# Attention with experts on one core: the experts' transposes and logits in the maxima's banks, P V in pairs of key blocks

## What is computed

```
xq, xk, xv = x @ wq.T, x @ wk.T, x @ wv.T          # (4, 1024, 16, 32)
probs = softmax(einsum('bqhd,bkhd->bhqk', xq, xk))
x = layernorm(x + (probs @ xv) @ wo.T)
logits = x @ Wr.T + br;  p = softmax(logits);  e = argmax(p)
h = einsum('nd,erd->ner', x, A);  y = einsum('ner,eor->neo', h, B) / 64
x = layernorm(x + y[e] * max(p))
```

## Time and profile before

| | us |
|---|---|
| median of three executions | 1601.32 |
| the profiled execution | 1602.13 |
| its span, first to last instruction | 1600.2 |
| TensorE busy | 1520.6 (95%) |
| POOL busy | 1184.0 (74%) |
| VectorE busy | 999.9 (62%) |
| ScalarE busy | 772.8 (48%) |

### The profile page before, as it was taken

How to read it: one execution, slowest core, us unless ns; L and a number is a source line. 1 busy time by engine, 2 the same in 40 slices (tenths; PEclk the granted TensorE clock), 3 DMA queues, 4 the chain that set the end, 5 groups by cost and what they waited for, 6 DMA issues and landing times.

```text
span 1600.2 us, 20249 instructions
## 1 busy us (share of the span) xinstructions
PE 1520.6 (95%) x6816; PEld 836.2 (52%) x6816; DVE 999.9 (62%) x1764; ACT 772.8 (48%) x1421; POOL 1184.0 (74%) x655
## 2 busy tenths in 40 slices
PE   6798979999999999999999999999999999999898
PEld 5664436666545555555644554555654444453354
DVE  5575576665586766656568667665556776672433
ACT  3154545555455454455545454544554545555222
POOL 0087889899977768777788876678877888889601
PEclk9898989999999999999999999999999999999999
DMA  7933334545232332237342133333433222210001
GB/s 230 295 99 97 99 105 139 153 140 142 84 99 64 83 93 76 71 100 221 96 146 47 58 89 87 83 110 104 171 90 100 48 47 58 57 41 21 7 1 53
DMA packets 79287, 156.27 MB, mean 98 GB/s; under 512 B 19008, under 2 KB 25168, under 8 KB 78800
## 3 DMA queue, kind: packets, MB, share of 16 engines
q1 hardware_dynamic: 77520, 152.33, 33.4%
q0 software_dynamic: 608, 2.12, 0.4%
q10 hardware_dynamic: 1056, 0.52, 0.1%
HBM read 105.66 MB, written 48.49 MB: 96 GB/s over the span
## 4 chain that ended last, share of the span: by engine, by line
PE 79%; DVE 8%; DMA 4%; issue 3%; SPq 2%; POOL 2%; ACT 1%; ACTq 0%; POOLq 0%; DVEq 0%
PE w L566 16%; PE sc L684 14%; PE pv L696 13%; PE mx L674 13%; PE w L643 5%; PE w L630 5%; PE w L601 5%; DVE mxc L885 3%; PE mx L655 2%; DMA stack<-qk_parts 2%; DVE xT_s L902 1%; PE w L623 1%; DVE gate L995 1%; DVE eq L990 1%; SPq L344 1%
## 5 line engine op out<-in xcount | busy, mean ns | idle before, releaser
L885 DVE TENSOR_REDUCE mxc<-mx 128x1 f32<-128x512 f32 x1024 | 680.7, 685 | 449.2 <-PE mx L674 447.5
L770 ACT ACTIVATE P<-sc 128x512 f32<-128x512 f32 x1024 | 594.6, 596 | 607.7 <-PE sc L684 592.5
L501 POOL TENSOR_TENSOR Psum<-Psum,P 128x1024 f32<-128x1024 f32 x300 | 711.0, 2396 | 45.7 <-ACT P L770 42.3
L684 PE MATMUL sc<-stack 98*128 98x512 f32 x1024 | 547.2, 536 | 7.7 <-ACT P L770 3.8
L674 PE MATMUL mx<-stack 96*128 96x512 f32 x1024 | 409.4, 403 | 26.5 <-DMA stack<-qk_parts 15.9
L684 PEld LDWEIGHTS sc<-stack 98*128 98x128 f32 x1024 | 195.3, 191 | 202.1 <-ACT P L770 94.8
L696 PE MATMUL pv<-P,V 128*32 128x512 f32 x2048 | 274.4, 608 | 0.0
L674 PEld LDWEIGHTS mx<-stack 96*128 96x128 f32 x1024 | 197.5, 193 | 130.8 <-issue 57.4
L566 PE MATMUL w<-xT_s,wqk_s 128*128 128x512 f32 x768 | 227.6, 411 | 20.8 <-DVE xT_s L902 13.2
L498 POOL TENSOR_TENSOR Psum<-P 128x1024 f32<-128x1024 f32 x50 | 117.8, 2376 | 147.8 <-PE mx L655 113.8
L566 PEld LDWEIGHTS w<-xT_s,wqk_s 128*128 128x128 f32 x768 | 144.2, 194 | 93.2 <-issue 55.2
(11 more groups left out here) (125 smaller groups left out, 1017.6 us busy)
## 6 DMA issues: line engine op xcount, KB each, us to landing
stack<-qk_parts SPq DMA_DIRECT2D x192, 256.0 KB, 5.5
qk_parts<-split SPq DMA_DIRECT2D x64, 512.0 KB, 3.2
wqk_s<-wqk_parts SPq DMA_DIRECT2D x30, 512.0 KB, 4.9
xT_s_f<-xT SPq DMA_DIRECT2D x8, 1024.0 KB, 11.2
den_s<-den_parts SPq DMA_DIRECT2D x124, 64.0 KB, 2.0
r<-x SPq DMA_DIRECT2D x3, 2048.0 KB, 9.4
out<-r SPq DMA_DIRECT2D x12, 512.0 KB, 3.9
wide<-wv_parts SPq DMA_DIRECT2D x2, 2048.0 KB, 12.0
```

Of the source, the lines that this page charges most:

```text
L501: pool.tensor_tensor(sums(s)[:, i, :], sums(s)[:, i, :], P[:, unit % NP, :], ALU.add).then_inc(add_done, 1)
L684: pe.matmul(sc[c][:, :], stack(s, i)[0:KS, 0, 128 * kb:128 * kb + 128], stack(s, i)[0:KS, 1, 512 * c:512 * c + 512], start=True, stop=True ...
L770: act.activation(P[:, unit % NP, 512 * c:512 * c + 512], sc[c][:, :], ACT.Exp).then_inc(exp_done, 1)
L885: dve.tensor_reduce(mxc[:, q % 2, m:m + 1], mx[TURN[g] % NMX][:, :], AX.X, ALU.max).then_inc(mx_done, 1)
```

## The change

Three edits, made together.

- **P V in pairs.** A new function `blocks(s, k)` says which key blocks are issued in unit k. In all slots but 7 it is two blocks in every fourth unit: blocks 0 and 1 in half 11, 2 and 3 in half 19, 4 and 5 in half 27, 6 and 7 in half 3 of the next slot. Slot 7 keeps one block every second unit.
- **Banks.** `t1`, `t2` and `lg` (`SHORT`) leave the order of the two `w` banks and take turns in the three `mx` banks. A turn now waits for whoever frees the turn three before: VectorE (`mx_done`), or ScalarE's copy after a `t1` or `t2`, or VectorE's bias add after a `lg`. The closing stage is as before.
- **Order of a tile's steps.** Before: lg, h, z of the tile before, t1 of the next, t2, then the projections. Now: z of the tile before, t2, lg of the next, projections, h of the next, t1 of the one after.

```diff
+    SHORT = ("t1", "t2", "lg")
...
-        pieces = [("t1", at)] + take(0) + [("lg", at), ("h", at), ("t1", at + 1)] + take(1) + [("t2", at)]
+        pieces = [("t1", at)] + take(0) + [("lg", at), ("h", at), ("t1", at + 1)] + take(1)
         for t in range(KB):
-            if t + 1 < KB:
-                pieces += [("lg", at + t + 1), ("h", at + t + 1)]
-            pieces += ([("z", at + t)] if t + 1 < KB else [])
-            if t + 2 < KB:
-                pieces.append(("t1", at + t + 2))
-            if t + 1 < KB:
-                pieces.append(("t2", at + t + 1))
-            pieces += take(t + 2)
+            pieces += ([("z", at + t - 1)] if t else []) + [("t2", at + t)]
+            pieces += ([("lg", at + t + 1)] if t + 1 < KB else []) + take(t + 2)
+            pieces += ([("h", at + t + 1)] if t + 1 < KB else []) + ([("t1", at + t + 2)] if t + 2 < KB else [])
         return pieces + fill + [("z", at + KB - 1)]
...
-        ORDER += PLAN[s]
+        ORDER += [piece for piece in PLAN[s] if piece[0] not in SHORT]
...
+    def next_turn(what):
+        TURN[what], FREES[what] = len(TURNS), frees + (what[0] not in SHORT)
+        TURNS.append(what)
+        return FREES[what]
...
         if s and h == den_at(s):
-            TURN["den", s - 1], turn = turn, turn + 1
-    TURNS = turn
+            frees = next_turn(("den", s - 1))
+        for kind, n, _ in AT.get(half, ()):
+            if kind in SHORT:
+                frees = next_turn((kind, n))
+
+    def blocks(s, k):
+
+        if s == PAIRS - 1:
+            return ((k - 3) // 2,) if k % 2 and k >= 3 else ()
+        return ((k - 5) // 2, (k - 3) // 2) if k % 4 == 1 and k >= 5 else ()
...
+        for turn, piece in enumerate(TURNS):
+            BANK[piece] = mx[turn % NMX]
...
+            def take_turn(what):
+
+                turn = TURN[what]
+                if turn >= NMX:
+                    old, n = TURNS[turn - NMX]
+                    if old in SHORT:
+                        pe.wait_ge(FREED_BY[old], n + 1)
+                    else:
+                        pe.wait_ge(mx_done, FREES[old, n])
+                return BANK[what]
+
             def begin(piece, last):
+                if not last and piece[0] in SHORT:
+                    return take_turn(piece)
...
-                if c == 1 and k == 1 and s:
-                    out_block(s - 1, KB - 1)
-                if c == 1 and k % 2 == 1 and k >= 3:
-                    out_block(s, (k - 3) // 2)
+                if c == 1 and s:
+                    for kb in blocks(s - 1, UNITS + k):
+                        if kb < KB:
+                            out_block(s - 1, kb)
+                if c == 1:
+                    for kb in blocks(s, k):
+                        out_block(s, kb)
```

More of the change, by code:

```diff
@@ L143, in den_at @@
         return 10 if second(s) != second(s - 1) or s % PAIRS == 2 else 6
-    TURN, turn = {}, 0
+    TURNS, TURN, FREES, frees = [], {}, {}, 0
+    def next_turn(what):
+        TURN[what], FREES[what] = len(TURNS), frees + (what[0] not in SHORT)
+        TURNS.append(what)
+        return FREES[what]
     for g in range(MAXES):
-        TURN[g], turn = turn, turn + 1
-    TURN["max_t", 0], turn = turn, turn + 1
+        frees = next_turn(("max", g))
+    frees = next_turn(("max_t", 0))
     for half in range(HALVES * SLOTS):
@@ L152, in build_attention_lora_moe_block @@
         for g in ITEMS[half]:
-            TURN[g], turn = turn, turn + 1
+            frees = next_turn(("max", g))
         if h == MAX_AT and s < LAST:
-            TURN["max_t", s + 1], turn = turn, turn + 1
+            frees = next_turn(("max_t", s + 1))
         if s and h == den_at(s):
-            TURN["den", s - 1], turn = turn, turn + 1
-    TURNS = turn
+            frees = next_turn(("den", s - 1))
[6 more added lines that the diff above has]
+        return ((k - 5) // 2, (k - 3) // 2) if k % 4 == 1 and k >= 5 else ()
     FIRST = KB * (B - 1)
@@ L384, in load_max @@
             def load_max(q):
-                sp.wait_ge(mx_done, TURN["max_t", q] + 1)
+                sp.wait_ge(mx_done, FREES["max_t", q])
                 for i in range(2):
@@ L391, in spread_den @@
             def spread_den(s):
-                sp.wait_ge(mx_done, TURN["den", s] + 1)
+                sp.wait_ge(mx_done, FREES["den", s])
                 if s:
@@ L648, in den @@
                 if bank is None:
-                    bank = mx[TURN["den", s] % NMX]
-                    pe.wait_ge(mx_done, TURN["den", s] - NMX + 1)
+                    bank = take_turn(("den", s))
                 pe.wait_ge(add_done, ADDS * (s + 1))
@@ L660, in max_t @@
                 pe.wait_ge(comb_done, q + 1)
-                turn = TURN["max_t", q]
-                pe.wait_ge(mx_done, turn - NMX + 1)
-                pe.transpose(mx[turn % NMX][0:2 * KB, 0:128], mm[:, :, :].rearrange("p i a -> p (i a)"), ident[:, :]).then_inc(mt_ready, 1)
+                bank = take_turn(("max_t", q))
+                pe.transpose(bank[0:2 * KB, 0:128], mm[:, :, :].rearrange("p i a -> p (i a)"), ident[:, :]).then_inc(mt_ready, 1)
             KIND = {"qk": qk, "v": v, "o": o, "part": part, "t1": t1, "lg": lg, "h": h, "t2": t2, "z": z, "den": den}
@@ L671, in max_item @@
                     pe.wait_ge((loaded0[q % 3], loaded1[q % 2])[i], 48 * (q // (3, 2)[i] + 1))
-                if TURN[g] >= NMX:
-                    pe.wait_ge(mx_done, TURN[g] - NMX + 1)
-                pe.matmul(mx[TURN[g] % NMX][:, :], stack(q, i)[0:3 * HD, 1, 128 * qb:128 * qb + 128],
+                bank = take_turn(("max", g))
+                pe.matmul(bank[:, :], stack(q, i)[0:3 * HD, 1, 128 * qb:128 * qb + 128],
                           stack(q, i)[0:3 * HD, 0, 512 * c:512 * c + 512], start=True, stop=True).then_inc(mx_ready, 1)
@@ L729, in _ @@
                     KIND[kind](n, chunk, bank)
-            out_block(LAST, KB - 1)
+            for kb in blocks(LAST, UNITS + 1):
+                out_block(LAST, kb)
             pe.wait_ge(exp_done, 2 * UNITS * SLOTS)
-            pe.wait_ge(mx_done, TURNS)
+            pe.wait_ge(mx_done, max(FREES.values()))
             for piece in CLOSING:
@@ L793, in copy_max @@
                     act.wait_ge(m_loaded, 64 * q)
-                act.activation(mrow[:, 0, :], mx[TURN["max_t", q] % NMX][0:2 * KB, 0:128], ACT.Copy).then_inc(mhi_done, 1)
+                act.activation(mrow[:, 0, :], BANK["max_t", q][0:2 * KB, 0:128], ACT.Copy).then_inc(mhi_done, 1)
             def copy_yT(n, bank):
@@ L884, in max_item @@
                 dve.wait_ge(mx_ready, g + 1)
-                dve.tensor_reduce(mxc[:, q % 2, m:m + 1], mx[TURN[g] % NMX][:, :], AX.X, ALU.max).then_inc(mx_done, 1)
+                dve.tensor_reduce(mxc[:, q % 2, m:m + 1], BANK["max", g][:, :], AX.X, ALU.max).then_inc(mx_done, 1)
                 if m == MAXES - 1:
-                    dve.wait_ge(mx_done, TURN[g] + 1)
+                    dve.wait_ge(mx_done, FREES["max", g])
                     if q:
@@ L894, in max_lo @@
                 dve.wait_ge(mhi_done, q + 1)
-                dve.tensor_tensor(mrow[:, 1, :], mx[TURN["max_t", q] % NMX][0:2 * KB, 0:128], mrow[:, 0, :].bitcast(f32),
+                dve.tensor_tensor(mrow[:, 1, :], BANK["max_t", q][0:2 * KB, 0:128], mrow[:, 0, :].bitcast(f32),
                                   ALU.subtract).then_inc(mx_done, 1)
@@ L916, in copy_den @@
                     dve.wait_ge(norm_done, 2 * s)
-                dve.tensor_copy(den_s[:, :], mx[TURN["den", s] % NMX][:, :]).then_inc(mx_done, 1)
+                dve.tensor_copy(den_s[:, :], BANK["den", s][:, :]).then_inc(mx_done, 1)
             def lo_part(n):
```

## The result

The change takes 1595.36 us in the median of 13 executions (1586.93 to 1599.91), the kernel before 1601.78 in the same runs. The ratio is 0.9948, 95% interval 0.9933 to 0.9963: half a per cent faster, 6.4 us, where 32 were forecast, and within 1%. The granted clock can account for most of the distance to the median: it was 0.976 on average here and 0.970 to 0.974 in the other twelve. From 0.976 to 0.972, that of the median execution, is 0.004 x 1590 x 2 = 13 us more at half clock, about 6 us of time. It isn't all, since the two executions that were faster still had only 0.973 and 0.974.

A forecast was written before the change was run, and what follows sets the result against it. It took TensorE (busy 95%, 79% of the chain of waits) as the bound, except where VectorE or POOL is full. 29.7 + 1.0 + 10.8 - 6.7 - 1.2 - 1.2 = 32.4 us saved, about 1569 us; range 1557 to 1588.

The forecast's parts named there:

- P V in pairs: Where TensorE is the bound, 106 of 124 pairs save 0.28 us each (0.26 to 0.32), 29.7 us.
- within 1%: Outcome class: measured time within 1% (16 us) of the kernel before; chance 0.10.
- Part 3: What gets worse, VectorE and the maxima's banks: 6.7 us more waits at gates, 1.2 us in slots 9 and 17.
- none of them stands in the four turns behind a gate, so I add nothing for that: Short steps bring TensorE one turn nearer to VectorE; none within four turns behind a gate, so 0 us added.
- I cost them at nothing: Added waits on ScalarE's copies of `t1` and `t2`: next turn over 1.5 us later, copy takes 0.6, so nothing.
- Part 2: TensorE's waits for a bank `w` between the experts' steps: all 10.8 us go.
- the 2.3 us for gates: Slots 26 to 28: gates of tiles 16, 18, 20 lose a block, 17 and 19 gain; 2.3 us more wait.
- the forecast of 2.2 us more: Slots 10 to 14: tiles 2 to 5 lose about 0.2 to 0.8 us each, 2.2 us more wait.
- 1.2 us for starving VectorE in 9 and 17: A pair and its chunk keep new blocks from VectorE for 3.5 us: 0.6 us in each slot, 1.2 us.
- The clock: Slot 2's longer pause may bring a second stretch at half clock, 1.2 us; slots 26 and 27 nothing.
- Rival C: Slots 10 to 30: pauses for the maxima's banks at each gate pull the clock down; slower, 1642 us; chance 6%.
- Rival A: VectorE sets the pace in the expert slots; every tile waits about 0.9 us more, 1584 us; chance 14%.

## Why the prediction was wrong

- **P V in pairs: right, undersized.** Forecast 0.28 us a pair with 0.26 to 0.32; measured 0.33. In slots 4 to 6, 1.33 us a slot. The Trainium skill's rule (TensorEngine Tiling (Array Packing), Key Properties), that a change of mode drains the array and a change of tile doesn't, was the better guide: the trace agrees, with nothing lost between the blocks (0.85 us for the second, two passes of 0.43). The second pass starting 0.46 us after the first instead of 0.43 was the block's own start, not a price of every pass.
- **The banks `w`: right.** All 10.8 us went, and it needed the third bank: the order alone kept 4.8 of 5.6 us in slots 10 to 16. It needed the order too: with the old one, 5.3 us of waits came back there, now for reductions.
- **Part 3's price for the waits of slots 26 to 30: the step that failed.** Forecast +0.9 us there from both parts (2.3 - 1.4), measured +10.8, and undoing banks and order in these slots gave 13.5 us back. Two terms of it were wrong. The first is "none of them stands in the four turns behind a gate, so I add nothing for that": it looked at gates only, and seven waits of 4.7 us stand behind the short steps themselves. With `t2` and `lg` in the ring, a logit step wants the bank of a block that started 1.3 us before, while VectorE adds z and takes its statistics (slot 28). With it fell "I cost them at nothing" of Part 2: the price was on VectorE's side, not ScalarE's. The second is the 2.3 us for gates, measured as 6.4. It moved the P V blocks around the gates and left the gates' length as it was, but the new order moved them against POOL's adds, and their two slow instructions went from 21.9 to 27.6 us.
- **The gates: the mechanism was right, the length was not.** A wait longer by "about 1.2 us" fits tiles 16 (1.45 before, 2.41 now) and 18 (1.30 and 2.46). Tile 20 had not waited and now waits 2.56, since its gates took 4.54 us instead of 2.90, and tile 23, for which nothing was forecast, waits 2.55. In slots 10 to 14 the forecast of 2.2 us more was too dark: the waits for reductions in slots 10 to 16 are 1.3 us in all, 0.9 before.
- **Slots 3, 9 and 17: undersized.** Their pairs were called lost, with 1.2 us for starving VectorE in 9 and 17; measured +3.9, and +4.4 for the two, 1.7 of it a fall of the clock in slot 9. Single blocks give nearly all of it back. A full VectorE does not only take the gain away. It wasn't starved either: in slot 17 its idle time stayed at 8 us and its splits of x took 1.9 us longer for 1.7 us of slot, as the gates did in slots 26 to 30. In slot 3, 1.2 us is the longer wait for the load in half 8 (8.3 instead of 7.1), which the prediction had seen and counted as made up for.
- **The clock: undersized.** Forecast 1.2 us, all in slot 2. Slot 2 kept its one stretch. Instead the profiled execution has 75.5 us at half clock where before had 57.3, and the median one about 89, some 16 us of time against the profiled one of before. "In slots 26 and 27 one fall more or less, nothing" became three more in slots 26 to 30, about 5 us. Rival C's mechanism came, at a fraction of its size. The Trainium skill's page TensorE: Matmul & The Clock Gate, section A second HAM failure mode, tells of a clock that swings when short idle times come between groups of matmuls; the trace agrees behind four pauses of 1.3 to 2.6 us in slots 26 to 30, and does not behind two of 2.46 and 1.58 us.
- **Range and rivals.** The time is above the range (1588). Rival A had the right engine, but spread its waits over the tiles of all expert slots; "within 1%" had 0.10. The rivals priced a wait a tile at a time, and none asked which slots lack filler for the banks. The total would be further off without errors the other way: slots 4 to 25 without 9 and 17 gained 34.0 us where 26.2 were forecast.

## What to carry to other kernels

Work of a narrow column group is worth issuing back to back, but only in stretches where TensorE itself is the bound; in slots 3, 9 and 17, where VectorE or POOL was full, it cost time, and in slots 26 to 30 it gave nothing. When pieces are moved into a shared ring of banks, count for each the time to the piece that wants the same bank, in the sparsest stretch of the program, and against everything its releaser has queued, not only the longest job. Where one engine's instructions lengthen another's, as POOL's adds did with VectorE's gates (0.2 to 2.2 us in most cases), a new order can change that length, and so it belongs into the price of the order. A change that leaves more short pauses should be priced with the clock that follows them.

## What the runs showed that was not expected

The clock also fell where TensorE had hardly paused. TensorE in slot 11 of the kernel with the experts of batch 2 as before, and the stretches ahead and behind:

```profile
574.18 0.60 PE L678 MATMUL mx<-ident,hm 128*128 128x128 f32 x4
...
575.47 1.06 PE L664 MATMUL mx<-wr_s,yT 128*128 128x8 f32 x8
...
577.32 0.50 PE L712 MATMUL mx<-stack 96*128 96x512 f32 x1 [0.45 <-DVE mxc L927]
```

```profile
574.90:578.30 3.40, 2.95 (x21) 1.60 (x23) 2.91 (x9) 1.74 (x4) 3.40 (x3) 1.00 0.00 0
578.50:581.70 3.20, 3.20 (x14) 1.05 (x7) 0.35 (x4) 0.00 (x0) 3.04 (x6) 0.50 0.05 10
```

A fall follows one pause of 0.45 us beside two transposes and a logit step with 8 columns, in slot 11 or 19 of seven of the kernels; the change's own profiled execution has the same instructions and the same pause there and no fall. So what follows such work differs from execution to execution, which may be part of the 13 us between the change's fastest and slowest. That thin work is the cause wasn't settled: the experiment that moved it apart changed too much else.
